# Reordering the setup of a two-layer convolution and attention kernel on one core

## Reference

```
# layer 0: x = x + conv0(_gn(x))
pooled = x.mean(axis=(2, 3))
h = relu(pooled @ ap_w1.T + ap_b1)
angles = tanh(h @ ap_w2.T + ap_b2) * (pi / 4)
w = bilinear rotation of base_kernel[G=8, 32, 32, 3, 3] by angles, one set per image
feat = grouped 3x3 convolution of x with w
out = feat * sigmoid(relu(pooled @ meta_w1.T + meta_b1) @ meta_w2.T + meta_b2)
# layer 1: x = x + attn(_gn(x))
q, k, v = xt @ Wq.T + bq, xt @ Wk.T + bk, xt @ Wv.T + bv   # xt: tokens x 256
scale = softplus(scale_param)        # q and k: relu, + 1e-6, / scale, cubed, norms kept
out = linear attention over 8 heads  # q (k^T v) / (q . sum k)
out = out + depthwise 5x5 convolution of v (dwc_w, dwc_b)
out = out @ Wproj.T + bproj
```

## Time and profile before

| what | value |
| --- | --- |
| median of 3 runs | 3930.86 us (3926.9 to 3932.67) |
| the profiled execution's own time | 3932.86 us |
| its span in the trace | 3930.8 us |
| TensorE busy (share of the span) | 3542.5 us (90%) |
| VectorE busy | 2972.1 us (76%) |
| ScalarE busy | 2711.0 us (69%) |
| GpSimd busy | 1426.4 us (36%) |
| granted TensorE clock, mean | 0.976 of full speed |

### The profile page before, as it was taken

The page is one execution under the profiler, slowest core; times in us unless marked ns, Lnnn a source line. Parts: engine busy times, 40 slices in busy tenths (PEclk is TensorE's granted clock), DMA queues, the critical chain, the costliest instruction groups (busy, mean ns, idle before and its releaser), DMA issues.

```text
span 3930.8 us, 96093 instructions
## 1 busy us (share of the span) xinstructions
PE 3542.5 (90%) x27980; PEld 2861.4 (73%) x27980; DVE 2972.1 (76%) x8235; ACT 2711.0 (69%) x7348; POOL 1426.4 (36%) x1318
## 2 busy tenths in 40 slices
PE   0569999999999999989999998999999899999797
PEld 0238777777877778777777877777787777778686
DVE  6767887868778786877868788786878878585756
ACT  2247776776777667676766767777677767677675
POOL 4632442514334252443514244351424425140302
PEclk9889999999999999999999999999999999999999
DMA  4672534536354462635436263443636354260302
GB/s 156 205 238 66 169 105 138 169 90 189 110 154 120 129 177 79 189 107 150 134 110 192 73 186 117 141 141 112 179 92 181 102 148 127 83 181 21 103 17 76
DMA packets 560048, 516.44 MB, mean 131 GB/s; under 512 B 97600, under 2 KB 491968, under 8 KB 559552
## 3 DMA queue, kind: packets, MB, share of 16 engines
q1 hardware_dynamic: 555200, 508.99, 43.9%
q10 hardware_dynamic: 4352, 1.57, 0.2%
HBM read 351.06 MB, written 134.22 MB: 123 GB/s over the span
## 4 chain that ended last, share of the span: by engine, by line
PE 42%; DVE 26%; issue 14%; ACT 13%; DMA 2%; DVEq 2%; SPq 1%; ACTq 0%; POOL 0%; POOLq 0%
PE F L1518 9%; PE VAB L1518 7%; PE F L1557 6%; ACT K L1295 6%; PE T L1529 5%; PE VAB L1557 5%; DVE F L975 4%; DVE XR L1064 3%; DVE XR L1057 3%; DVE XHL L969 3%; DVE XR L1046 2%; ACT K L1301 2%; PE PP L1608 2%; DVE ST L962 1%; DVE RATIO L989 1%
## 5 line engine op out<-in xcount | busy, mean ns | idle before, releaser
L1518 PE MATMUL F<-WQ,XHL 128*128 128x256 f16 x6144 | 822.7, 275 | 27.3 <-ACT V L1335 19.0
L650 POOL TENSOR_TENSOR XR<-XR,V 128x512 f32<-128x512 f32 x256 | 326.0, 1274 | 1038.9 <-DVE XR L1046 1038.9
L1518 PEld LDWEIGHTS F<-WQ,XHL 128*128 128x128 f16 (+1 forms) x6144 | 603.4, 99 | 105.6 <-issue 33.6
L1295 ACT ACTIVATE K<-F,SCAL 128x256 f32<-128x256 f32 x1024 | 476.3, 471 | 292.3 <-DVE F L975 279.7
L1504 PE MATMUL SM<-SL,BD 128*128 128x512 f16 x2688 | 634.9, 385 | 0.0
L634 POOL TENSOR_TENSOR SL<-PL,SL 128x1122 f16<-128x1122 f32 x112 | 260.1, 2322 | 1031.8 <-DVE SL L947 1031.8
L1301 ACT ACTIVATE K<-K,SCAL 128x256 f32<-128x256 f32 x1024 | 514.0, 510 | 160.9 <-DVE K L981 160.8
L981 DVE TENSOR_TENSOR K<-K,F 128x512 f32<-128x512 f32 x512 | 351.6, 687 | 282.0 <-ACT K L1295 184.0
L975 DVE TENSOR_TENSOR F<-F,FL 128x512 f32<-128x512 f32 x512 | 353.9, 691 | 154.4 <-PE F L1520 148.3
L1504 PEld LDWEIGHTS SM<-SL,BD 128*128 128x128 f16 x2688 | 261.0, 97 | 284.1
L1608 PE MATMUL PP<-XR,WP 128*128 128x256 f16 x3072 | 388.9, 278 | 67.8 <-DVE XR L1064 67.8
(11 more groups left out here) (194 smaller groups left out, 6954.6 us busy)
## 6 DMA issues: line engine op xcount, KB each, us to landing
XR<-xr SPq DMA_DIRECT2D x132, 512.0 KB, 5.3
U<-x SPq DMA_DIRECT2D x256, 256.0 KB, 3.8
XR<-x SPq DMA_DIRECT2D x256, 256.0 KB, 4.1
out<-XR SPq DMA_DIRECT2D x256, 256.0 KB, 3.8
PL<-xp SPq DMA_DIRECT2D x112, 561.0 KB, 3.8
RX<-xr SPq DMA_DIRECT2D x118, 512.0 KB, 4.0
x<-RX SPq DMA_DIRECT2D x448, 128.0 KB, 2.1
BD<-RX SPq DMA_DIRECT2D x240, 96.0 KB, 2.2
```

What stands on the lines that cost most here:

```text
L650: g_.tensor_tensor(o, o, fm, ALU.add).then_inc(o_rdy, 2)
L1295: a.activation(K2[:, p, ts], F[p][:, ts], ACT.Square, scale=inv_a, accum_out=S2[:, 2 * p + t:2 * p + t + 1]).then_inc(f_sq, 1)
L1518: t_.matmul(o, XHL[:, xa, h, at], WQ[:, wa, h, c0:c0 + C], start=(k == 0), stop=False)
```

## The change

It moves and rewrites setup work; batches keep their code but for one wait.

- SP loads the eight statistics tiles of image 0 first, then layer 0's constants. Those of layer 1 come later, behind the first four statistics tiles of image 1. Taps are loaded into `PL` and `SL` (three tiles, free until image 2) in place of `U2` and `K23` (four). Statistics tiles 0 and 1 of image 2 are loaded before `weights(0)`.
- VectorE starts with `pixel_stats(0, g)`. `softplus`, `largest_weights`, `largest_biases` and `scales` move behind the norms of image 0 or of image 1.
- `partition_all_reduce` goes. A new `largest(k)` turns the four columns of maxima by a product with the identity, reduces on VectorE, and spreads the result by a second product with ones. It runs twice, for the kernels and for the other weights.
- The high halves of `WQ`, `WP` and the biases are made on ScalarE, behind the new wait for `ready`; VectorE makes the low halves with one operation each, inside the first convolution.
- Three chunks of taps get their high half before the first convolution. All 12 low halves are made inside it, one after each half group from the third on; before, four stood ahead of it. TensorE waits for them (`tp_rdy`) ahead of the depthwise product, and not ahead of the first keys.

Declarations of semaphores are left out of the diff.

```diff
@@ -228,7 +229,7 @@
-        N_W, N_C = 8, 8
+        N_W, N_C = 5, 8
@@ -249,11 +250,14 @@
+        MOST = VT[:, :, :, :, :].rearrange("p a b c d -> p (a b c d)")
+        ONE4, DIAG, TOP = MOST[0:4, 0:P], MOST[0:4, P + 2:P + 6], MOST[0:4, P + 8:P + 9]
...
-            return U2[:, i % 2, :] if i % 4 < 2 else KS[:, i % 2, :]
+            return PL[:, 0:PIX] if i % 3 == 0 else SL[:, i % 3 - 1].rearrange("p a n -> p (a n)").bitcast(f32)[:, 0:PIX]
@@ -338,10 +342,10 @@
             def load_taps(i):
-                if i >= 4:
-                    sp.wait_ge(tp_dve, i - 3)
+                if i >= 3:
+                    sp.wait_ge(tp_rdy, i - 2)
                     carry(sp)
-                sp.dma_start(taps_tile(i), toeplitz[:, i * PIX:(i + 1) * PIX]).then_inc(taps_in[i % 4], 16)
+                sp.dma_start(taps_tile(i), toeplitz[:, i * PIX:(i + 1) * PIX]).then_inc(taps_in[i % 3], 16)
@@ -406,9 +410,9 @@
                 for g in range(GROUPS):
-                    if g < 4:
-                        load_taps(2 * g + 4)
-                        load_taps(2 * g + 5)
+                    if 1 <= g <= 5:
+                        for i in (2 * g + 1, 2 * g + 2)[:CHUNKS - 2 * g - 1]:
+                            load_taps(i)
@@ -427,10 +431,6 @@
-                    load_stats(2, g)
-                sp.wait_ge(tp_dve, CHUNKS)
-                carry(sp)
-                for g in (0, 1):
@@ -451,6 +451,8 @@
                             next_unit(0, u)
+                sp.wait_ge(tp_rdy, CHUNKS)
+                carry(sp)
@@ -513,14 +515,8 @@
-            sp.dma_start(sc32, head_scale[0, :].partition_broadcast(P)).then_inc(w_in, 16)
-            sp.dma_start(wq32, wqkv.rearrange("(h p) n -> p h n", p=P)).then_inc(w_in, 16)
-            sp.dma_start(bq32, bqkv[0, :].partition_broadcast(P)).then_inc(w_in, 16)
-            sp.dma_start(wp32, wproj.rearrange("(h p) n -> p h n", p=P)).then_inc(w_in, 16)
-            sp.dma_start(dt32, dw_taps[0, :].partition_broadcast(P)).then_inc(w_in, 16)
-            sp.dma_start(DWB[:, :], dw_b[0, :].partition_broadcast(P)).then_inc(w_in, 16)
-            sp.dma_start(BP[:, :], bproj).then_inc(w_in, 16)
-            sp.dma_start(BPC[:, :], bproj_patch).then_inc(w_in, 16)
+            for g in range(GROUPS):
+                load_stats(0, g)
@@ -529,27 +525,33 @@
             sp.dma_start(GRID[:, :, :, :, :].rearrange("p i k h t -> p (i k h t)"), grid).then_inc(c_in, 16)
-            for g in range(GROUPS):
-                load_stats(0, g)
...
                 load_planes(0, g)
+            sp.dma_start(sc32, head_scale[0, :].partition_broadcast(P)).then_inc(sc_in, 16)
...
                 load_stats(1, g)
-            sp.wait_ge(s0_rdy, 12)
-            carry(sp)
-            for i in range(4):
-                load_taps(i)
+            sp.dma_start(dt32, dw_taps[0, :].partition_broadcast(P)).then_inc(t_in, 16)
+            sp.dma_start(DWB[:, :], dw_b[0, :].partition_broadcast(P)).then_inc(t_in, 16)
+            sp.dma_start(wq32, wqkv.rearrange("(h p) n -> p h n", p=P)).then_inc(w_in, 16)
+            sp.dma_start(bq32, bqkv[0, :].partition_broadcast(P)).then_inc(w_in, 16)
+            sp.dma_start(wp32, wproj.rearrange("(h p) n -> p h n", p=P)).then_inc(w_in, 16)
+            sp.dma_start(BP[:, :], bproj).then_inc(w_in, 16)
+            sp.dma_start(BPC[:, :], bproj_patch).then_inc(w_in, 16)
...
                 load_stats(1, g)
-            weights(0)
+            for i in range(3):
+                load_taps(i)
...
                 load_pixels(0, g)
+            for g in (0, 1):
+                load_stats(2, g)
+            weights(0)
@@ -676,15 +678,12 @@
             g_.memset(BD[:, :, :, :, :], 0.0).then_inc(set_pool, 1)
-            pool.wait_ge(set_dve, 1)
-            g_.partition_all_reduce(SCAL[:, 0:4], S6[:, 0:4], P, RMAX).then_inc(set_pool, 1)
...
                 conv_low(0, g)
-            rotation(1, lambda j: conv_low(0, 3 + j // 2) if j in (0, 2, 4, 6) else None)
-            conv_low(0, 7)
+            rotation(1, lambda j: conv_low(0, 3 + j // 2) if j % 2 == 0 else None)
@@ -710,8 +709,9 @@
-            for t in (ONES, BQ, KVS, HID, NOT, ST):
+            for t in (ONES, BQ, KVS, HID, NOT, ST, S6):
...
+            setup(v.memset(ONE4, 1.0))
@@ -728,10 +728,18 @@
                                       apply_absolute_value=True))
-                dve.sem_inc(set_dve, 1)
+            def largest(k):
+                dve.sem_inc(most_rdy, 1)
+                dve.wait_ge(most_mm, 2 * k + 1)
+                setup(v.tensor_reduce(TOP, PP[0:4, 0:P], AX.X, ALU.max))
+                setup(v.tensor_scalar(DIAG, MATS[0:4, 0, 0:4], TOP, None, ALU.mult))
+                dve.sem_inc(most_rdy, 1)
+                dve.wait_ge(most_mm, 2 * k + 2)
+                setup(v.tensor_copy(SCAL[:, 0:4], SM[:, 64:68]))
             def scaled_kernels():
-                dve.wait_ge(set_pool, 2)
@@ -772,12 +780,16 @@
+            def largest_taps():
+                dve.wait_ge(t_in, 32)
...
                 over(a_t, m_t, 16384.0)
+                dve.sem_inc(t_rdy, 1)
@@ -804,21 +816,21 @@
-            def split(src, hi, lo, a):
-                setup(v.tensor_scalar(src, src, a, None, ALU.mult))
-                setup(v.tensor_copy(hi, src))
-                setup(v.tensor_tensor(lo, src, hi, ALU.subtract))
-            def split_bias():
-                split(bq32, bh16, bl16, a_w)
-                setup(v.tensor_copy(BQ[0:1, :], bh16[0:1, :]))
-                setup(v.tensor_copy(BQ[32:33, :], bl16[32:33, :]))
+            def split(k, src, hi, lo, a):
+                dve.wait_ge(hi_rdy, k + 1)
+                setup(v.scalar_tensor_tensor(lo, src, a, hi, ALU.mult, ALU.subtract))
...
-                                       ALU.mult, ALU.subtract).then_inc(tp_dve, 1)
+                                       ALU.mult, ALU.subtract).then_inc(tp_rdy, 1)
+            def split_bias():
+                split(3, bq32, bh16, bl16, a_w)
+                setup(v.tensor_copy(BQ[0:1, :], bh16[0:1, :]))
+                setup(v.tensor_copy(BQ[32:33, :], bl16[32:33, :]))
@@ -1146,35 +1158,37 @@
-            dve.wait_ge(w_in, 16 * N_W)
-            softplus()
-            largest_weights()
+            for g in range(GROUPS):
+                pixel_stats(0, g)
...
             largest_kernel()
-            for g in range(GROUPS):
-                pixel_stats(0, g)
+            largest(0)
...
             take_norms(0)
+            for g in range(4):
+                pixel_stats(1, g)
...
                 high(0, g)
-            largest_biases()
-            scales()
-            for g in range(GROUPS):
+            dve.wait_ge(sc_in, 16)
+            softplus()
+            for g in range(4, GROUPS):
...
             tail(1, 1)
-            for h in range(HALVES):
-                split(wq32[:, h, :], WQ[:, 0, h, :], WQ[:, 1, h, :], a_w)
-            for i in range(4):
-                low_taps(i)
+            largest_taps()
+            dve.wait_ge(w_in, 16 * N_W)
+            largest_weights()
+            largest(1)
+            largest_biases()
+            scales()
@@ -1184,12 +1198,14 @@
                         take_norms(1)
-                    if q == 1 and g == 0:
+                    if q == 1 and g < 2:
+                        split(g, wq32[:, g, :], WQ[:, 0, g, :], WQ[:, 1, g, :], a_w)
+                    if q == 1 and g == 2:
+                        split(2, wp32, WP[:, 0], WP[:, 1], a_p)
+                    if q == 1 and g == 3:
                         split_bias()
-                    if q == 1 and g == 1:
-                        split(wp32, WP[:, 0], WP[:, 1], a_p)
-                    if 2 <= g < 6:
-                        low_taps(2 * g + q)
+                    if 2 <= 2 * g + q < 2 + CHUNKS:
+                        low_taps(2 * g + q - 2)
@@ -1251,8 +1267,8 @@
-            def high_taps(i):
-                act.wait_ge(taps_in[i % 4], 16 * (i // 4 + 1))
+            def taps(i):
+                act.wait_ge(taps_in[i % 3], 16 * (i // 3 + 1))
@@ -1399,29 +1415,33 @@
-            exponentials()
...
-            act.wait_ge(ready, 1)
-            for i in range(4):
-                high_taps(i)
+            exponentials()
...
+            act.wait_ge(t_rdy, 1)
+            for i in range(3):
+                taps(i)
+            act.wait_ge(ready, 1)
+            for k, (hi, src, s) in enumerate(((WQ[:, 0, 0, :], wq32[:, 0, :], a_w), (WQ[:, 0, 1, :], wq32[:, 1, :], a_w),
+                                              (WP[:, 0], wp32, a_p), (bh16, bq32, a_w))):
+                a.activation(hi, src, ACT.Copy, scale=s).then_inc(hi_rdy, 1)
...
-                if 2 <= g < 6:
-                    high_taps(2 * g)
-                    high_taps(2 * g + 1)
...
+                if 2 <= g <= 6:
+                    for i in (2 * g - 1, 2 * g)[:CHUNKS - 2 * g + 1]:
+                        taps(i)
@@ -1455,6 +1475,12 @@
+            def largest(k):
```

(8 more changed lines are left out.)

9 lines of the change are left out of this document (5 added, 4 removed).

## The result

| what | before | after |
| --- | --- | --- |
| median of 8 runs each, same chips | 3925.86 us (3913.98 to 3932.67) | 3888.22 us (3881.2 to 3907.17) |
| ratio, 95% interval | | 0.9914 [0.9893, 0.9936] |
| span of the profiled execution | 3930.8 us | 3881.2 us |
| its own time, mean granted clock | 3932.86 us, 0.976 | 3882.95 us, 0.981 |
| first `conv_out` | 118.99 us | 95.38 us |

The kernel became faster, by 0.86%. Both have to be explained.

A forecast was written before the change was run, and what follows sets the result against it. The prologue's chain ahead of TensorE's first convolution was taken as what bounds, with VectorE's setup the bound after the change. 26 − 3.9 − 8.4 + 5 + 3 = 21.7, say 22 us: median 3930.86 becomes 3909, range 3896 to 3921.

The forecast's parts named there:

- The early part: Start of the prologue: statistics first, maxima by TensorE, scaling; kernels scaled at 20.7 us, image 0's sines at 34.2, against 52.36.
- The 6.7 us on GpSimd: Pause ahead of GpSimd's first rotation multiply; might go with the all-reduce, but the sum let it stay.
- VectorE becomes the bound: Up to the first `conv_out`: VectorE's setup ends at 93 us (86 to 100), after TensorE's bank at 90.5; 26 us earlier.
- The 13 operations: Two-input operations of `softplus` and `largest_weights`, now beside GpSimd's rotation: 0 to 11 us of delay, taken as 4.5.
- The first convolution: Its stretch: wait for planes −3.9 us, four more low halves of taps −8.4, splits even within 1, 5 given back.
- My back-payment of 5 us: First convolution: half of about 10 us in which VectorE idled behind its first `conv_out`, given back as +5 us.
- The second convolution: VectorE's 3.00 us idle for tile 0 of image 2 goes through the earlier load: +3 us.
- the batches keep their length: The batches after the prologue, 3648 us: claimed to keep their length, a change of nothing.
- Larger: Rival, 3902 to 3896 us: two-input operations hardly meet GpSimd and taps get cheaper, gain 34.5 us; chance 0.13.
- Smaller: Rival, 3915 to 3925 us: `ready` at 100 or tap loads wait in the first convolution; chance 0.17.
- no effect: Rival, 3931 us: setup still precedes the first `conv_out`, needing `ready` at 115 us; chance 0.06.
- slower: Rival, 3945 us: the ring of three tap tiles sets the first convolution's pace through slow landings; chance 0.06.

The follow-up runs named there:

- old_order_products: The kernel before, in its own order, with the two products of `largest(0)` in place of the all-reduce; 3922.84 us against 3921.2, ratio 1.0003.
- reduce_kept: The changed kernel with GpSimd's all-reduce again for the kernels' maximum; 3897.13 us, ratio 0.9923 to the kernel before.
- splits_dve: The changed kernel with splits of `WQ`, `WP` and biases as three VectorE operations each, no high halves of weights on ScalarE; 3917.84 us in one run.
- thin_taps2: The changed kernel with 15 of 16 of the taps' low halves left out, zeros filled by GpSimd after image 1's rotation; 3889.4 us in one run.
- late_k: The changed kernel with statistics tiles 0 and 1 of image 2 loaded behind the second convolution's weights again; 3895.93 us in one run.
- pad24: The changed kernel with 32 unused VectorE reductions, 24 us of delay, ahead of the first batch; 3925.71 us, ratio 0.9997 to the kernel before.

## Why the prediction was right and wrong

**The early part.** `c_in` 16 us, measured 16.95; `largest(0)` 2.2, measured 2.3; kernels scaled at 20.7, measured 21.47; last sine at 34.2, measured 35.44. These steps hold to 1.3 us.

**The 6.7 us on GpSimd.** Here I chose wrongly, and it cost the sum nothing, as was said. They went with the all-reduce, in the changed kernel and in `old_order_products` alike, and came back with it in `reduce_kept`. By the Trainium skill (GPSIMD Engine Reference, Instruction dispatch) the first call to a freshly loaded kernel costs about 6 us with no visible instruction. The 6.9 us of the kernel before agree in size, the 9.4 us of `reduce_kept` are half as much again, and no row shows what fills either pause. What I had not seen is the sign: an earlier rotation lies on top of more of VectorE's setup. Nor did the earlier rotation bring TensorE's first product forward: it ended at 72.63 and not at 76.6, but the product came at 89.01, where 85.1 was forecast, behind ScalarE's half of the weights, which the sum did not have.

**VectorE becomes the bound.** Right: `scales` ended at 95.11 where 93 was forecast, and VectorE met a full bank. The net is 6.7 us over my 88.4, where I had added 4.5, but not by the terms I had. The 13 operations lost 5.3 us, near the 4.5 and well under the 9 of the estimate from the port lock. Five one-input operations of `softplus`, which I had put at nothing, lost 3.3 more, up to 1.25 us from 0.28. Against it, my 13.8 us for biases, taps and `scales` had been read beside the rotation and held contention already; away from it they took 10.8. These two errors of 3 us cancelled, and 1.1 us of a later start and of stretched heads remained. The first `conv_out` came 23.6 us earlier and not 26.

**The first convolution.** Forecast 7.3 us longer, measured 3.85. The wait for planes was 3.55 (forecast 3.9). Twelve low halves of taps took 22.8 us where eight had taken 16.9, 5.9 more and not 8.4. The splits, which I had put at even, took 8.2 us of six operations in this stretch before and take 4.1 now; `splits_dve` shows that the form is worth 6 us. My back-payment of 5 us was a guess with the right sign: 3.55 + 5.9 − 4.1 = 5.35, and 1.5 of it came back. The premise that VectorE's work is the length of the stretch is only partly true (`thin_taps2`).

**The second convolution.** Forecast +3, measured 4.5 from 82.96 to 78.45; `late_k` has 3.0 of it as the wait.

**The sum.** 22 us forecast, 24.2 measured at the start of the batches. VectorE became the bound, as forecast. The closeness of the sum is in part luck: the early part was 2.4 us short of its 26, and the two convolutions gave 5.0 us more than forecast.

**The step that failed** is the last one, from the prologue to the program's time: "the median 3930.86 becomes 3909", with a range made of the prologue's unknowns alone. Of the 20.8 us by which 3888.22 lies below 3909, 5.0 are the kernel before, which ran at 3925.86 and not 3930.86 once it was timed beside the changed one; 2.2 are the prologue; and 13.6 lie outside it, in what I had put at nothing with "the batches keep their length", without a width for it. Their instructions do, but in the profiled pair they are 25.4 us shorter, with 132.0 − 93.0 = 39.0 us less at the lower clock. Half of that, 19.5 us, is what it is worth by estimate. Whether the clock also gave the 13.6 us of the medians stays open: for that comparison the clocks of the kernel before are not on record, and in the other two the clock was against the change. Two further comparisons gave 3904.96 and 3892.57, one inside the range. That the change gave the batches a lasting gain is neither shown nor shut out by `pad24`. The mean of the three comparisons, 29.1 us, is 6 us more than the landmarks account for, and medians of the same kernel lie 16.7 us apart; so the cause of this remainder stays open.

**The rivals.** *Larger* had a gain of up to 34.5 us, and 37.6 were measured, but not by its mechanism: GpSimd met VectorE's operations more than I thought. *Smaller*, *no effect* and *slower* did not occur. The ring of taps, *slower*'s mechanism, exists (ScalarE waits 25.2 us in all for tiles), but landings stayed at 8.3 us or less and VectorE waited for taps for only 3.3.

## What to carry to other kernels

When work is taken out from ahead of a path, look for which engine becomes the bound, and price what it then runs beside: here the move was worth 24 us, and the all-reduce that looked like a cost kept GpSimd away from VectorE for 9.4 us, so that its removal put the batches some 5 us later in the new order and gave nothing in the old one. A duration read beside a busy neighbour holds that neighbour's share; it is not the price of the same work elsewhere. A range for a whole program has to hold the scatter of the part that is not changed: here 3.6 ms of batches moved the median by 17 us between comparisons, more than most terms of the sum. Landmarks in the profile (first multiply, first `conv_out`, first keys) settle steps of 1 to 5 us that the program's time can't.

## What the runs showed of the hardware

- A two-input VectorE operation that started while GpSimd ran a two-input instruction ended behind it, however small it was: by 0.08 us with 64 columns (eight times), by 1.08 with 1024 (seven times). 64 columns took 0.53 to 2.22 us so and 0.27 otherwise. The Trainium skill (SBUF — State Buffer, SBUF: two separate sides) describes the shared pair of ports as a lock held for a whole instruction; these rows agree.
- Some one-input operations pay as well: a `tensor_scalar` of 256 columns took up to 1.25 us from 0.28, one of 4x4 took 8.72 beside a memset of 20.58. Reciprocals (1.75 us) and statistics (4.85 us for eight) took the same beside the rotation as without it, and a two-input operation on 64 columns took 0.28 beside a memset.
- The pause ahead of GpSimd's first multiply after an all-reduce was 6.9 us in one kernel and 9.4 in another, and 0.25 us with no all-reduce.
- The mean granted clock of one kernel went from 0.975 to 0.981 over eight runs, and its time from 3907.17 to 3881.2 us.
